# Ending the first block of a cross attention after one pair's key copies, and moving projection units one tile earlier in a wide attention

## The chip, the cores and the metric

The kernel runs on one core of a Trainium2 chip as a single program. The metric is the device time of one execution in microseconds; the time of a version is the median over several executions. Besides those, one execution was profiled; all views below read that one.

## The reference, cut to what matters

A perceiver-like stack of two layers over x (16 batches of 64 tokens, 256 features). Layer 0 does a cross attention to a context of 1601 rows with 16 heads of 16, then a "wide" attention with 8 heads of 128 over 1024 tokens and 1024 context rows, then a feed-forward with merged task weights. Layer 1 does a shared-key cross attention, an attention with position slopes, and a mixture of experts. Only these two attentions are touched:

```python
# cross attention, per batch of 64 tokens and per head (16 of 16 features)
qh = split(layernorm(x) @ wq + bq);  kh = split(ctx @ wk + bk);  vh = split(ctx @ wv + bv)
out = softmax(qh @ kh.T / 4) @ vh;   x = x + out @ wo + bo
# wide attention, per head (8 of 128 features), all 1024 tokens against all 1024 context rows
qh = split(layernorm(x) @ Wq);  kh = split(context @ Wk);  vh = split(context @ Wv)
sim = (qh @ kh.T) * 128 ** -0.5;  sim = (sim - mean(sim)) * 1.5 + mean(sim)
x = x + softmax(sim) @ vh @ Wout + bout
```

## The kernel before, in words

Every stage of the kernel is a block (`core.block()`, line 47) that holds one hand-written program for each engine: SyncE issues the transfers, TensorE multiplies, VectorE, ScalarE and GpSimd do the rest, and semaphores order them. A block ends when all its engine programs have ended; no engine starts the next block earlier. A transfer that was only issued need not have landed by then; who needs it waits on its semaphore.

**Cross attention** (`cross_attention_block`). `first_block` (line 556) normalises x, projects the queries of all batches, stores them to a scratch tensor in DRAM, and makes the keys and values of batch 0 in 17 projection units: 8 units of keys (4 for each of two groups of 4 head pairs), 7 of values, one of keys shared with layer 1, one that turns these. For each unit TensorE fills a PSUM bank (`project`), VectorE moves it out (`move_projection`), and for keys GpSimd splits it into a rounded and a rest part (`split_keys`). SyncE then copies the parts from SBUF to SBUF into the stacked layout `k_stack` (`stack_keys(n)`, line 446, four transfers of 200 KB for one head pair n; there are 8 pairs), and the queries into `q_stack` (`load_q`, line 439, eight transfers of 32 KB for one batch). `store_shared` (line 452) is eight transfers, `load_ctx` and `store_values` one each.

The main block then runs over 16 batches. In batch b TensorE goes through the 8 pairs; per pair it computes scores in two halves, turns the probabilities of the pair before, and does two projection units of batch b+1 in between. Each projection needs the bank `projected` moved out before. VectorE runs through the same order: maximum of the first score half, move of unit 2n, maximum of the second half, move of unit 2n+1. The move of the first key unit of a group overwrites `k_part`, from which `stack_keys` copies, and so waits until all four pairs of that group are stacked (in `move_projection`):

```python
if s == 0 and b > 0:
    for pair in range(GROUP_PAIRS * g, GROUP_PAIRS * (g + 1)):
        dve.wait_ge(k_stacked[pair], 64 * b)
```

**Wide attention** (`wide_attention_block`, line 1040). Eight heads one after the other; a head has eight tiles of 128 tokens (t = 0 to 7), and queries, keys and values of head h+1 are projected in six units (two of queries, two of keys, two of values) while head h runs. TensorE's order in tile t is: scores of t; at t = 1 the weighing of the last four tiles of the head before, at t = 5 that of the first four of its own (`weigh`); from t = 2 on unit t-2; then the turn of tile t-1's probabilities. VectorE: maximum of t; keeping what was weighed (t = 1 and 5); `normalise(t)`, which waits for ScalarE's exponential of t; from t = 2 on the move of unit t-2. ScalarE: exponential of t, then the copy of turned tile t-1. All six units share one bank, so unit u+1 waits for the move of u, and a head starts with a wait for the move of its own last unit: `pe.wait_ge(projection_moved, U * h + U)`. `over_heads` (line 1080) writes out heads 0, 1, 6 and 7 and runs heads 2 to 5 as a hardware loop of two rounds with two heads each; SyncE's weight loads are a loop of three rounds.

Of the kernel before, what the change touches and what calls it, by code (L numbers as in the profile page):

```python
# [26 lines left out]
PAIRS = HEADS // 2  # L27
GROUP_PAIRS = 4
# [356 lines left out]
def cross_attention_block(core, layer, x, wo, wk, wv, bk, bv, bo, w_shared, b_shared, scratch, heads_t):  # L385
# [15 lines left out]
    with ExitStack() as stack:  # L401
# [33 lines left out]
        def load_ctx(sp, b, parity):  # L435
            sp.dma_start(ctx[parity][:], dram["ctx_t"][ds(b, 1)].rearrange("o p c n -> (o p) c n")).then_inc(ctx_loaded[parity], 16)

        def load_q(sp, b, parity):
            for copy in range(COPIES):
                for e in range(2):  # L440
                    row = copy * PAIR_ROWS + e * HEAD_DIM
                    sp.dma_start(q_stack[parity][row:row + HEAD_DIM, :, e, :].bitcast(F32),
                                 scratch[copy // 2].rearrange("c (p e d) n -> e d (c p) n", e=2, d=HEAD_DIM)[e, :, :, ds(b * SEQ, SEQ)]
                                 ).then_inc(q_loaded[parity], 16)
# [111 lines left out]
        def first_block(first):  # L556
# [34 lines left out]
            with core.block() as block:  # L591
                @block.sync
                def _(sp):
                    for i in range(HALVES):
                        half = slice(i * TILES // 2, (i + 1) * TILES // 2)
                        sp.dma_start(x[:, half], dram["x"][:, half]).then_inc(x_loaded[i], 16)
                    sp.dma_start(core.ident[:], dram["ident"]).then_inc(ident_loaded, 16)
                    sp.dma_start(wk[:], dram[f"{layer}_wk"]).then_inc(keys_loaded, 16)
                    sp.dma_start(bk[:], dram[f"{layer}_bk"]).then_inc(keys_loaded, 16)
                    sp.dma_start(w_shared[:], dram["L1_xattn_wkv"]).then_inc(keys_loaded, 16)  # L600
                    sp.dma_start(b_shared[:], dram["L1_xattn_bkv"]).then_inc(keys_loaded, 16)
                    load_ctx(sp, 0, 0)
                    sp.dma_start(wq[:], dram[f"{layer}_wq"]).then_inc(query_loaded, 16)
                    sp.dma_start(bq[:], dram[f"{layer}_bq"]).then_inc(query_loaded, 16)
                    sp.dma_start(wv[:], dram[f"{layer}_wv"]).then_inc(values_loaded, 16)
                    load_ctx(sp, 1, 1)
                    for tile, view in ((core.even_head, dram["even_head"]), (core.odd_head, dram["odd_head"]), (bv, dram[f"{layer}_bv"]),
                                       (wo, dram[f"{layer}_wo"]), (bo, dram[f"{layer}_bo"].partition_broadcast(P))):
                        sp.dma_start(tile[:], view).then_inc(others_loaded, 16)
                    for i, (m, half) in enumerate(q_units):  # L610
                        for part, ready in ((0, high_ready), (1, low_ready)):
                            sp.wait_ge(ready, i + 1)
                            sp.dma_start(scratch[part, m, :, half * BANK:(half + 1) * BANK],
                                         parts[part][:, m, half * BANK:(half + 1) * BANK].bitcast(F32)).then_inc(query_stored, 16)
                    sp.wait_ge(zeros_ready, 4)
                    sp.wait_ge(query_stored, 16 * 2 * len(q_units))
                    load_q(sp, 0, 0)
                    load_q(sp, 1, 1)
                    for n in range(PAIRS):
                        if n % GROUP_PAIRS == 0:  # L620
                            sp.wait_ge(keys_split, CHUNKS_PER_GROUP * (n // GROUP_PAIRS + 1))
                        stack_keys(sp, n)
                        if n == GROUP_PAIRS - 1:
                            store_shared(sp, 0)
                    sp.wait_ge(projection_done, U)
                    load_ctx(sp, 2, 0)
                    store_values(sp, 0, 0)
                    sp.wait_ge(others_loaded, 16 * 5)

                @block.gpsimd  # L630
# [148 lines left out]
        with core.block() as block:  # L779
            @block.sync  # L780
            def _(sp):
                def batch(b, parity, ctx_left, q_left):

                    for n in range(PAIRS):
                        if n % GROUP_PAIRS == 0:
                            sp.wait_ge(keys_split, K_UNITS * (b + 1) + CHUNKS_PER_GROUP * (n // GROUP_PAIRS + 1))
                        sp.wait_ge(scored, 2 * (PAIRS * b + n + 1))
                        stack_keys(sp, n)
                        if n == GROUP_PAIRS - 1:
                            store_shared(sp, b + 1)  # L790
                    if q_left:
                        load_q(sp, b + 2, parity)
                    if ctx_left:
                        sp.wait_ge(projection_done, U * (b + 2))
                        load_ctx(sp, b + 3, 1 - parity)
                    store_values(sp, b + 1, 1 - parity)

                for b in range(BATCH - 1):
                    batch(b, b % 2, b < BATCH - 3, b < BATCH - 2)
                sp.wait_ge(shared_stored, 2 * CHUNKS_PER_GROUP * 16 * BATCH)  # L800
                for i in range(2):
                    sp.wait_ge(values_stored[i], 8 * BATCH)
# [237 lines left out]
def wide_attention_block(core, xn_t, ctx, w_q, w_k, w_v, wout, bout, heads_t):  # L1040
# [6 lines left out]
    with ExitStack() as stack:  # L1047
# [29 lines left out]
        weighed_ready = sem("weighed_ready")  # L1077
        heads_ready = sem("heads_ready")

        def over_heads(eng, body):  # L1080
            body(0, 0, True, False)
            body(1, 1, False, False)
            with eng.Fori(1, WIDE_HEADS // 2 - 1) as j:
                body(2 * j, 0, False, False)
                body(2 * j + 1, 1, False, False)
            body(WIDE_HEADS - 2, 0, False, False)
            body(WIDE_HEADS - 1, 1, False, True)

        with core.block() as block:
            @block.sync  # L1090
            def _(sp):
                def load(h, parity):
                    for tile, name in ((w_q, "L0_attn_wq"), (w_k, "L0_attn_wk"), (w_v, "L0_attn_wv")):
                        sp.dma_start(tile[parity][:], dram[name][ds(h, 1)].rearrange("o p c n -> (o p) c n")).then_inc(weights_loaded[parity], 16)

                sp.dma_start(bout[:], dram["L0_attn_bout"].partition_broadcast(P)).then_inc(out_loaded, 16)
                sp.dma_start(wout[:], dram["L0_attn_wout"]).then_inc(out_loaded, 16)
                with sp.Fori(0, WIDE_HEADS // 2 - 1) as j:
                    for parity in range(2):
                        used = sp.snap(U * (2 * j + parity + 1))  # L1100
                        sp.wait_ge(projection_done, used)
                        load(2 * j + parity + 2, parity)
                sp.wait_ge(out_loaded, 32)

            @block.gpsimd
# [5 lines left out]
            def _(pe):  # L1111
# [49 lines left out]
                def head(h, parity, first, last):  # L1161
                    pe.wait_ge(projection_moved, U * h + U)
                    for t in range(TILES):
                        score(h, parity, t)
                        if t == 1 and not first:
                            weigh(h - 1, 1 - parity, 1)
                        if t == QUERY_TILES + 1:
                            weigh(h, parity, 0)
                        if not last and 2 <= t:
                            project(h + 1, 1 - parity, t - 2)  # L1170
                        if t > 0:
                            turn(h, t - 1)
                        elif not first:
                            turn(h - 1, TILES - 1)

                for u in range(U):
                    project(0, 0, u)
                over_heads(pe, head)
                turn(WIDE_HEADS - 1, TILES - 1)
                weigh(WIDE_HEADS - 1, 1, 1)  # L1180

# [1 line left out]
            def _(dve):  # L1183
# [34 lines left out]
                def head(h, parity, first, last):  # L1218
                    for t in range(TILES):
                        maximum(h, t)  # L1220
                        if t == 1 and not first:
                            keep_heads(h - 1, 1)
                        if t == QUERY_TILES + 1:
                            keep_heads(h, 0)
                        normalise(h, t)
                        if not last and 2 <= t:
                            move_projection(h + 1, 1 - parity, t - 2)

                for u in range(U):
                    move_projection(0, 0, u)  # L1230
                over_heads(dve, head)
                keep_heads(WIDE_HEADS - 1, 1)

            @block.scalar
            def _(act):
# [21 lines left out]
                        elif not first:  # L1257
                            move_turned(h - 1, TILES - 1)

                over_heads(act, head)  # L1260
                move_turned(WIDE_HEADS - 1, TILES - 1)


# [1393 lines left out]
```

## Time and profile before

| | us |
|---|---|
| median of 3 executions | 2504.31 (2503.99 to 2508.21) |
| the profiled execution, its own time | 2509.65 |
| its span in the trace | 2507.8 |
| first block of the cross attention ends on TensorE's side | about 49 |
| main block of the cross attention starts | about 81 |
| wide attention's block, first scores to last weighing | 960.9 to about 1350 |

The span is what the trace covers; 1.85 us of the execution's own time lie around it. "PE" is TensorE's matmuls, "PEld" its weight loads, "DVE" VectorE, "ACT" ScalarE, "POOL" GpSimd, "SPq" the issue of transfers by SyncE. A matmul group "x4" for two matmuls in the code is what fp32 operands cost in passes. In a timeline the first number is the start, the second how long the merged group lasted, and square brackets tell how long the engine had been idle and who released it.

### The profile page before, as it was taken

The numbers are of one execution on the slowest core, as the hardware profiler recorded it, in microseconds if no ns is written. First come the engines' busy times: TensorE is split into PE (matmuls) and PEld (weight loads), VectorE is DVE, ScalarE is ACT, GpSimd is POOL, SyncE is SP. The second block draws the span as 40 slices with busy tenths as digits, with TensorE's granted clock in tenths as the row PEclk, the third lists the DMA queues.
The fourth block names the chain that finished last, engine by engine and source line by source line (L and its number), as shares of the span: only waits on it lengthen the run. The fifth ranks groups of instructions, "written<-read, shape, count | busy, mean of one in ns | idle before, by whom it ended". The sixth has DMA issues, their size and how long they took to land. (4 is left out here: it accounts for less than half of the span.)

```text
span 2507.8 us, 39287 instructions
## 1 busy us (share of the span) xinstructions
PE 2203.5 (88%) x15444; PEld 1472.6 (59%) x15444; DVE 1261.2 (50%) x2221; ACT 1000.1 (40%) x1861; POOL 310.8 (12%) x353
## 2 busy tenths in 40 slices
PE   5699999999999878999998799958999997685694
PEld 3477777777777754455555587834555544444463
DVE  3455665656566534454442344356777734564113
ACT  1355555555555533333331011115666653241221
POOL 2233222232223100000000000050000001000102
PEclk9899999999999969999999799968999999795897
DMA  6667777677777600000000312051222203115112
GB/s 186 139 144 180 177 179 172 154 180 179 180 162 167 146 23 26 11 6 5 5 1 1 125 69 100 18 104 22 26 31 34 34 1 86 39 18 209 61 45 67
DMA packets 107749, 220.09 MB, mean 88 GB/s; under 512 B 58818, under 2 KB 75211, under 8 KB 101844
## 3 DMA queue, kind: packets, MB, share of 16 engines
q1 hardware_dynamic: 106036, 213.44, 35.5%
q0 software_dynamic: 1536, 4.20, 0.5%
q8 instruction: 122, 2.00, 0.3%
q14 instruction: 55, 0.45, 0.1%
HBM read 91.08 MB, written 19.27 MB: 44 GB/s over the span
## 5 line engine op out<-in xcount | busy, mean ns | idle before, releaser
L905 DVE TENSOR_REDUCE L_xattn_maxima<-L_xattn_scores 128x1 f32<-128x1024 f32 (+1 forms) x256 | 253.7, 991 | 245.5 <-PE L_xattn_scores L828 245.0
L972 ACT ACTIVATE L_xattn_probs_t<-L_xattn_turned 128x1024 f32<-128x1024 f32 (+1 forms) x256 | 220.6, 862 | 339.1 <-PE L_xattn_turned L840 339.1
L1763 DVE TENSOR_REDUCE shared_half_maxima<-shared_ring 128x1 f32<-128x1024 f32 (+1 forms) x256 | 248.9, 990 | 107.0 <-PE shared_ring L1677 103.4
L1836 ACT ACTIVATE shared_exps<-shared_scores 128x512 f32<-128x512 f32 (+1 forms) x416 | 225.6, 594 | 123.6 <-PE shared_scores L1698 122.9
L984 ACT ACTIVATE L_xattn_probs<-L_xattn_scores,L_xattn_maxima 128x1024 f32<-128x1024 f32 (+1 forms) x256 | 235.4, 925 | 38.0 <-DVE L_xattn_maxima L908 38.0
L840 PE MATMUL L_xattn_turned<-ident,L_xattn_probs 128*128 128x128 f32 x1664 | 236.2, 282 | 12.2 <-ACT L_xattn_probs_t L972 11.2
L840 PEld LDWEIGHTS L_xattn_turned<-ident,L_xattn_probs 128*128 128x128 f32 x1664 | 199.1, 145 | 79.4 <-issue 46.7
L828 PE MATMUL L_xattn_scores<-L_xattn_k_stack,L_xattn_q_stack 128*128 128x512 f32 (+1 forms) x512 | 160.9, 396 | 50.7 <-DVE L_xattn_fold L958 33.2
L506 PE MATMUL L_xattn_projected<-L_xattn_wv,L_xattn_ctx 128*128 128x256 f32 x780 | 193.6, 389 | 0.0
L500 PE MATMUL L_xattn_projected<-L_xattn_ctx,L_xattn_wk 128*128 128x400 f32 x480 | 182.3, 502 | 0.0
L1698 PE MATMUL shared_scores<-shared_q,shared_k 128*128 128x512 f32 (+1 forms) x416 | 154.7, 450 | 7.3 <-DMA shared_q<-shared_max_rows 7.1
L1677 PE MATMUL shared_ring<-shared_k,shared_q 128*128 128x512 f32 (+1 forms) x512 | 139.8, 374 | 22.1 <-DMA shared_q<-q_scratch 12.8
L506 PEld LDWEIGHTS L_xattn_projected<-L_xattn_wv,L_xattn_ctx 128*128 128x128 f32 x780 | 137.2, 187 | 21.3 <-issue 0.3
L1252 ACT ACTIVATE wide_probs<-wide_scores,wide_stats 128x1024 f32<-128x1024 f32 x64 | 71.3, 1114 | 163.6 <-DVE wide_stats L1202 163.6
L469 POOL CAST L_xattn_k_part<-L_xattn_k_part 128x400 fp32r<-128x400 f32 (+1 forms) x128 | 66.2, 517 | 555.6 <-DVE L_xattn_k_part L530 555.6
L1379 PE MATMUL ffn_merging<-ffn_spread,ffn_task 128*128 128x256 f32 x512 | 129.5, 404 | 5.0 <-DVE ffn_merged L1458 5.0
L471 POOL TENSOR_TENSOR L_xattn_k_part<-L_xattn_k_part 128x400 fp32r<-128x400 f32 (+1 forms) x128 | 132.6, 1036 | 10.2
L1712 PE MATMUL shared_weighed<-shared_exps,shared_v 128*32 128x256 f32 (+1 forms) x1664 | 132.9, 391 | 0.2 <-ACT shared_exps L1836 0.2
L1137 PE MATMUL wide_scores<-wide_k_t,wide_q_t 128*128 128x512 f32 x256 | 122.2, 600 | 11.3 <-DVE wide_v L1192 11.3
L1677 PEld LDWEIGHTS shared_ring<-shared_k,shared_q 128*128 128x128 f32 x512 | 98.0, 201 | 48.2 <-DVE shared_half_maxima L1763 16.9
L828 PEld LDWEIGHTS L_xattn_scores<-L_xattn_k_stack,L_xattn_q_stack 128*128 128x128 f32 x512 | 79.6, 196 | 77.5 <-issue 42.8
L1157 PE MATMUL wide_weighed<-wide_probs_t,wide_v 128*128 128x512 f32 x256 | 116.0, 607 | 10.3 <-ACT wide_probs_t L1243 10.3
(368 smaller groups left out, 3065.4 us busy)
## 6 DMA issues: line engine op xcount, KB each, us to landing
L_xattn_k_stack<-L_xattn_k_part SPq DMA_DIRECT2D x512, 200.2 KB, 4.2
L_xattn_ctx<-in_ctx_t SPq DMA_DIRECT2D x16, 1602.0 KB, 6.9
ffn_task<-in_ffn_task SPq DMA_DIRECT2D x16, 1024.0 KB, 6.7
experts_w_in<-in_expert_in SPq DMA_DIRECT2D x8, 1024.0 KB, 11.6
shared_k<-k_scratch SPq DMA_DIRECT2D x64, 100.1 KB, 4.2
L_xattn_q_stack<-q_scratch SPq DMA_DIRECT2D x128, 32.0 KB, 2.0
k_scratch<-L_xattn_shared_part SPq DMA_DIRECT2D x128, 32.0 KB, 1.7
shared_q<-q_scratch SPq DMA_DIRECT2D x64, 64.0 KB, 4.6
```

The source lines that it names most:

```text
L500: last = nc.tensor.matmul(bank[:, 0:w], wk[:, k, g * P:(g + 1) * P], ctx[parity][:, k, s:s + w], start=k == 0, stop=k == CHUNKS - 1)
L506: last = nc.tensor.matmul(bank[0:rows, i * DIM:(i + 1) * DIM], ctx[parity][:, k, t * P:t * P + rows], wv[:, k, :], start=k == 0, stop=k == ...
L828: last = nc.tensor.matmul(scores[:, s // BANK, 0:w], q_stack[parity][:, n].rearrange("p h q -> p (h q)"), k_stack[:, n, s:s + w], start=Tr ...
L840: last = nc.tensor.transpose(turned_tiles[:, i, :], probs[n % 2][:, t * P:(t + 1) * P], core.ident[:])
L905: nc.vector.reduce_max(maxima[n % 2][:, half:half + 1], cols, axis=AX).then_inc(halves_maxed, 1)
L972: nc.scalar.activation(probs_t[:, t:t + m, p * P:(p + 1) * P], turned_tiles[:, 0:m, :], ACT.Copy).then_inc(turned_moved, 1)
L984: nc.scalar.activation(probs[n % 2][:, lo:hi], scores_flat[:, lo:hi], ACT.Exp, bias=maxima[n % 2][:, 2:3], scale=SCALE, accum_out=sums[n / ...
L1677: last = nc.tensor.matmul(ring[:, s // BANK, 0:w], q[slot][:, 2 * n:2 * n + 2, :].rearrange("r h q -> r (h q)"), k[slot][:, s:s + w], star ...
L1698: nc.tensor.matmul(scores[0:m, h, :], k[slot][:, t * P:t * P + m], q[slot][:, h * 8:(h + 1) * 8, :].rearrange("r h q -> r (h q)"), start=T ...
L1712: last = nc.tensor.matmul(weighed[b % 2][32 * c:32 * (c + 1), 0, 0:TILE_COLS], v[0:m, b, t, :], exps[n % 2][0:m, c * TILE_COLS:(c + 1) * T ...
L1763: nc.vector.reduce_max(half_maxima[:, n, half:half + 1], ring_flat[:, HALF_STARTS[half]:HALF_STARTS[half + 1]], axis=AX).then_inc(ring_max ...
L1836: nc.scalar.activation(exps[n % 2][0:m, h * BANK:(h + 1) * BANK], scores[0:m, h, :], ACT.Exp, scale=SCALE).then_inc(exps_done, 1)
```

## The change

In the cross attention, the SyncE program of the first block now ends after the queries of batch 0 and the keys of the first pair are on their way. The stacking of pairs 1 to 7, the shared store, the queries of batch 1, the context of batch 2 and the store of the shared values are issued at the start of SyncE's program in the main block, in this new order.

In the wide attention, projection unit t-1 is done in tiles 1 to 6 (before: unit t-2 in tiles 2 to 7), ahead of the weighing in that tile; VectorE moves it right after the maximum, ahead of keeping the weighed tile and of `normalise`. The loops over heads and over weight loads are written out for all engines.

```diff
@@ first_block, SyncE
                     load_q(sp, 0, 0)
-                    load_q(sp, 1, 1)
-                    for n in range(PAIRS):
-                        if n % GROUP_PAIRS == 0:
-                            sp.wait_ge(keys_split, CHUNKS_PER_GROUP * (n // GROUP_PAIRS + 1))
-                        stack_keys(sp, n)
-                        if n == GROUP_PAIRS - 1:
-                            store_shared(sp, 0)
-                    sp.wait_ge(projection_done, U)
-                    load_ctx(sp, 2, 0)
-                    store_values(sp, 0, 0)
+                    sp.wait_ge(keys_split, CHUNKS_PER_GROUP)
+                    stack_keys(sp, 0)
                     sp.wait_ge(others_loaded, 16 * 5)
@@ main block, SyncE
+                for n in range(1, PAIRS):
+                    if n == GROUP_PAIRS:
+                        store_shared(sp, 0)
+                        sp.wait_ge(keys_split, K_UNITS)
+                    stack_keys(sp, n)
+                load_q(sp, 1, 1)
+                sp.wait_ge(projection_done, U)
+                load_ctx(sp, 2, 0)
+                store_values(sp, 0, 0)
                 for b in range(BATCH - 1):
@@ wide attention, over_heads
-        def over_heads(eng, body):
-            body(0, 0, True, False)
-            body(1, 1, False, False)
-            with eng.Fori(1, WIDE_HEADS // 2 - 1) as j:
-                body(2 * j, 0, False, False)
-                body(2 * j + 1, 1, False, False)
-            body(WIDE_HEADS - 2, 0, False, False)
-            body(WIDE_HEADS - 1, 1, False, True)
+        def over_heads(body):
+            for h in range(WIDE_HEADS):
+                body(h, h % 2, h == 0, h == WIDE_HEADS - 1)
@@ SyncE
-                with sp.Fori(0, WIDE_HEADS // 2 - 1) as j:
-                    for parity in range(2):
-                        used = sp.snap(U * (2 * j + parity + 1))
-                        sp.wait_ge(projection_done, used)
-                        load(2 * j + parity + 2, parity)
+                for h in range(2, WIDE_HEADS):
+                    sp.wait_ge(projection_done, U * (h - 1))
+                    load(h, h % 2)
@@ TensorE, head
                         score(h, parity, t)
+                        if not last and 1 <= t <= U:
+                            project(h + 1, 1 - parity, t - 1)
                         if t == 1 and not first:
                             weigh(h - 1, 1 - parity, 1)
                         if t == QUERY_TILES + 1:
                             weigh(h, parity, 0)
-                        if not last and 2 <= t:
-                            project(h + 1, 1 - parity, t - 2)
@@ VectorE, head
                         maximum(h, t)
+                        if not last and 1 <= t <= U:
+                            move_projection(h + 1, 1 - parity, t - 1)
                         if t == 1 and not first:
                             keep_heads(h - 1, 1)
                         if t == QUERY_TILES + 1:
                             keep_heads(h, 0)
                         normalise(h, t)
-                        if not last and 2 <= t:
-                            move_projection(h + 1, 1 - parity, t - 2)
```

## Rows read from the trace of the kernel before

**Rows 1.** The page, busy time of each engine and its share of the span.
```profile
PE 2203.5 (88%) x15444; PEld 1472.6 (59%) x15444; DVE 1261.2 (50%) x2221; ACT 1000.1 (40%) x1861; POOL 310.8 (12%) x353
```

**Rows 2.** Timeline around the block boundary: start, duration, engine, line, what.
```profile
49.20 0.16 DVE L553 COPY L_xattn_v_shared<-L_xattn_first_projected 65x16 f32<-65x16 f32 x1
...
81.12 0.48 DVE L956 MEMSET L_xattn_projected<- 128x512 f32 x1 [31.75 <-PEq L50]
...
82.09 1.19 PE L828 MATMUL L_xattn_scores<-L_xattn_k_stack,L_xattn_q_stack 128*128 128x512 f32 x2 [33.20 <-DVE L_xattn_fold L958]
...
85.99 0.63 DVE L530 TENSOR_SCALAR L_xattn_k_part<-L_xattn_projected,L_xattn_bk 128x400 f32<-128x400 f32 x1 [1.44 <-PE L_xattn_projected L500]
...
109.21 0.64 DVE L530 TENSOR_SCALAR L_xattn_k_part<-L_xattn_projected,L_xattn_bk 128x400 f32<-128x400 f32 x1
```

**Rows 3.** Timeline of SyncE's issues over the same boundary and into batch 0.
```profile
36.86 7.44 SPq L442 DMA_DIRECT2D L_xattn_q_stack<-q_scratch  x16
44.34 14.60 SPq L449 DMA_DIRECT2D L_xattn_k_stack<-L_xattn_k_part  x16
...
63.81 14.63 SPq L449 DMA_DIRECT2D L_xattn_k_stack<-L_xattn_k_part  x16
...
79.50 0.96 SPq L461 DMA_DIRECT2D v_scratch<-L_xattn_v_shared  x1
105.96 14.61 SPq L449 DMA_DIRECT2D L_xattn_k_stack<-L_xattn_k_part  x16
```

**Rows 4.** One tile's instructions, k_stack, in 44.2 to 54.6: twelve issues, and landing.
```profile
L449 SPq DMA_DIRECT2D L_xattn_k_stack<-L_xattn_k_part x12: 580/923/1024, 44.3 to 54.0; - x12
...
DMA to landing us min/median/max: 2.9/4.1/4.3
```

**Rows 5.** Timeline of TensorE in the wide attention, tiles inside heads and at head changes.
```profile
1120.01 1.88 PE L1137 MATMUL wide_scores<-wide_k_t,wide_q_t 128*128 128x512 f32 x4
1121.99 1.98 PE L1119 MATMUL wide_projected<-wide_xn_t,wide_w_q 128*128 128x512 f32 x4
...
1144.56 1.88 PE L1137 MATMUL wide_scores<-wide_k_t,wide_q_t 128*128 128x512 f32 x4
...
1150.92 1.98 PE L1137 MATMUL wide_scores<-wide_k_t,wide_q_t 128*128 128x512 f32 x4 [1.53 <-DVE wide_v L1192]
...
1156.78 7.13 PE L1157 MATMUL wide_weighed<-wide_probs_t,wide_v 128*128 128x512 f32 x16 [1.29 <-ACT wide_probs_t L1243]
...
1164.62 1.88 PE L1137 MATMUL wide_scores<-wide_k_t,wide_q_t 128*128 128x512 f32 x4
1166.34 1.88 PE L1119 MATMUL wide_projected<-wide_xn_t,wide_w_q 128*128 128x512 f32 x4
...
1205.62 7.13 PE L1157 MATMUL wide_weighed<-wide_probs_t,wide_v 128*128 128x512 f32 x16 [1.22 <-ACT wide_probs_t L1243]
...
1254.31 7.13 PE L1157 MATMUL wide_weighed<-wide_probs_t,wide_v 128*128 128x512 f32 x16 [1.14 <-ACT wide_probs_t L1243]
...
1302.99 7.13 PE L1157 MATMUL wide_weighed<-wide_probs_t,wide_v 128*128 128x512 f32 x16 [1.13 <-ACT wide_probs_t L1243]
```

**Rows 6.** Timeline of the last head, which projects nothing: tiles 2 to 4.
```profile
1310.84 1.88 PE L1137 MATMUL wide_scores<-wide_k_t,wide_q_t 128*128 128x512 f32 x4
...
1316.54 1.08 PE L1147 MATMUL wide_turned<-ident,wide_probs 128*128 128x128 f32 x8 [1.23 <-DVE wide_probs L1210]
1317.45 1.88 PE L1137 MATMUL wide_scores<-wide_k_t,wide_q_t 128*128 128x512 f32 x4
...
1319.00 1.01 ACT L1243 ACTIVATE wide_probs_t<-wide_turned 128x1024 f32<-128x1024 f32 x1
```

**Rows 7.** Timeline of TensorE in the first head, tiles 1 and 2.
```profile
966.64 1.74 PE L1147 MATMUL wide_turned<-ident,wide_probs 128*128 128x128 f32 x8 [2.02 <-DVE wide_probs L1210]
968.18 2.96 PE L1137 MATMUL wide_scores<-wide_k_t,wide_q_t 128*128 128x512 f32 x4
970.97 1.88 PE L1119 MATMUL wide_projected<-wide_xn_t,wide_w_q 128*128 128x512 f32 x4
```

More of the change, by code:

```diff
@@ L1177, in _ @@
                     project(0, 0, u)
-                over_heads(pe, head)
+                over_heads(head)
                 turn(WIDE_HEADS - 1, TILES - 1)
@@ L1225, in head @@
                         normalise(h, t)
-                        if not last and 2 <= t:
-                            move_projection(h + 1, 1 - parity, t - 2)
                 for u in range(U):
                     move_projection(0, 0, u)
-                over_heads(dve, head)
+                over_heads(head)
                 keep_heads(WIDE_HEADS - 1, 1)
@@ L1258, in head @@
                             move_turned(h - 1, TILES - 1)
-                over_heads(act, head)
+                over_heads(head)
                 move_turned(WIDE_HEADS - 1, TILES - 1)
```

## The prediction

> **What bounds the kernel now.** I read the page first: TensorE is busy 88% of the span [rows 1], and the stages run one after the other, so time can only come out of stretches in which TensorE stands. The timeline around the first boundary shows the largest: VectorE's last work of the first block ends at 49.36, the main block starts at 81.12, TensorE's first scores come at 82.09 after 33.2 us of nothing [rows 2]. SyncE's own timeline tells why: it issues transfers without a pause from 36.86 to 80.46, and the block ends 0.66 us later (81.12 less 79.50 and 0.96) [rows 2, 3]. So the boundary is set by SyncE's issuing, not by any result. In the wide attention the reader is to see short waits instead: 1.53 us at a head's start, for VectorE's move of the last value unit, and 1.29 us ahead of the weighing in tile 1, for ScalarE's copy [rows 5].
>
> **Part 1, the end of the first block.** SyncE now issues 8 query transfers instead of 16 and 4 key copies. From the rows the 8 take half of 7.44, to 40.6, and the first pair's four 3.7 at most (a quarter of 14.60), to 44.3 [rows 3]. The block then ends with VectorE, at 49.36; plus the same 0.66 the main block starts at 50.0, and by the same 0.97 TensorE's first scores at 51.0. That alone would be worth 31.1 us.
>
> But a wait takes over. VectorE's second instruction in batch 0 is the move of the first key unit of batch 1, into the buffer from which pairs 0 to 3 are copied, and it waits for all four to have landed. Before, pair 3 was issued by 58.94 and VectorE got there at 85.99 [rows 2, 3], so the wait cost nothing. Now pairs 1 to 3 are issued from 50.1 on. Twelve such issues go from 44.3 to the start of the last at 54.0, 9.7 us, and one takes 4.1 (at most 4.3) to land [rows 4]: 50.1 + 9.7 + 4.2 = 64.0, and the move starts at 64.1 instead of 85.99. Queued behind it are the maximum of the second score half, hence both exponentials, and on TensorE unit 1, which waits for the bank, and everything after it. So the main chain is 21.9 us early, not 31.1.
>
> Of this the clock takes something back. TensorE does one projection and the scores from 51.0 on, then stands for some 10 us until 64.7. In the trace, work right after an idle time of 2.0 us is at the lower level: from 966.64 to 970.97, 4.33 us for a turn and a score pair [rows 7], which warm take 0.91 (1316.54 to 1317.45) and 1.72 (1164.62 to 1166.34) [rows 5, 6], so 1.7 lost. Before, such a slow stretch lay ahead of 85.99, thus inside what is already counted; now one comes behind the move. I take 1.7, with 0 (the slow stretch falls into ScalarE's first exponential) and 3.5 (two such stretches) as ends. Part 1 gives 21.9 - 1.7 = 20.2 us, from 18 to 22.
>
> Is anything late next? The group-1 keys of batch 1 are moved at 109.21 [rows 2], now 89.0. They wait for pairs 4 to 7: SyncE is through pair 3 at 60.7, the shared store of 4.9 (58.94 to 63.81) brings it to 65.6, the 16 issues of 14.63 to 80.2 [rows 3], landed by 83.6: 5 us of slack. Then 8 query issues (3.7), the context and the values (78.44 to 80.46, 2.0) end at 85.9 [rows 3]. The next stacking, for batch 1, waited for GpSimd until 105.96 [rows 3], now 85.8, and so is not delayed by more than 0.2; its reader comes with batch 1, tens of us later. Every moved issue is thus under computation. If SyncE's issues were a fifth slower beside computing, group 1 would land near 88; still in time.
>
> **Part 2, the wide attention.** Take a change of heads, from tile 7's scores to the weighing in tile 1. Before: 1144.56 to 1156.78, 12.22 us, with one projection unit and both waits in it [rows 5]. After: tile 7 has no unit, its scores are followed by one turn and the next head's scores, which need wait no longer, since the last unit was moved in tile 6. But now the turn of tile 7 comes too soon for its own probabilities. The last head shows this very order without a projection: scores at 1310.84, turn of the same tile at 1316.54, 1.23 us of it idle; next scores at 1317.45 [rows 6]. So 5.70 + 0.91, then scores 1.72 and the unit that now stands in tile 1, another 1.72 [rows 5] (the unit's own length taken as that of the scores, four matmuls of the same shape): 10.05. ScalarE's copy for the weighing is done 9.17 us after the scores of tile 7 (1319.00 + 1.01 less 1310.84) [rows 6], hence hidden. Gain 2.17 us, at the six changes from head 0 to head 6.
>
> At the seventh, head 7 has no unit in tile 1: the weighing waits for that copy, at about 9.35, and the unit taken out of tile 7 (1.72) still has to be done before: 12.22 - 9.35 - 1.72 leaves 1.1 us.
>
> Bank waits inside a head: the second query unit began 1.98 after the scores instead of 1.72 (1120.01 to 1121.99) [rows 5], since VectorE moved the first behind `normalise`. Moved right after the maximum, this goes: 0.26 for each of seven heads, 1.8 us.
>
> Head 0 stands 2.02 us before its first turn and then runs slow, 1.7 us lost as above [rows 7]. The unit in tile 1 fills 1.6 of that idle time (the turn itself waits for VectorE's normalising and stays where it is), and with 0.4 idle the slow stretch should go: 3.3 us, or 1.6 if it stays.
>
> VectorE's order could cost: the move now stands ahead of `normalise`. But `normalise` waits for ScalarE's exponential, which can start only behind the maximum, and the move falls into that time. It lasts 0.63 for 400 columns [rows 2], by which I estimate 0.8 for 512. I count nothing; uncovered it would be up to 0.8 a tile (rival C).
>
> The loops: four heads change from loop to straight code. Inside the loop a head took 48.84 (1156.78 to 1205.62), outside 48.68 (1254.31 to 1302.99) [rows 5], 0.2 us apart, and this lies in the waits just removed: no term of its own, 0 to 0.8 us. The Trainium skill (Runtime: NRT & Kernel Launch, Instruction fetch mechanics) says that a taken branch out of the fetched window stalls until its page is fetched, and that prefetching is sequential; by it the written-out loop would gain, and the trace allows that at most these 0.2 us a head.
>
> Part 2: 6 x 2.17 = 13.0, + 1.1 + 1.8 + 3.3 = 19.2 us, from 15 to 21.
>
> **Sum.** 20.2 + 19.2 = 39.4 us off the profiled execution's 2509.65, 2470.3. The profiled one stood 5.3 us above the median; nothing in the removed time is particular to it, so the same is taken off the median: 2504.3 - 39.4 = 2464.9 us.
>
> **Rivals.**
> A: the wait for pairs 0 to 3 does not bind, and the whole 31.1 us come. For it: only that the boundary gap is that long. Against: the wait is in the code and the landing time in the rows. 2504.3 - 31.1 - 19.2 = 2454.0. 4%.
> B: TensorE's clock falls at the new wait ahead of tile 7's turn, at each of seven head changes. Each costs 1.7 [rows 7], 12 us in all: 2476.8. Against it: the last head has this wait of 1.23 us and behind it runs a turn in 1.08 and scores in 1.88, warm [rows 6]; idle times of 1.53 were followed by warm work too [rows 5]. 8%. The Trainium skill (TensorE: Matmul & The Clock Gate, "A second HAM failure mode: psum-queue depth-cycling") tells of frequent short idle times in which the clock keeps falling; that is this rival.
> C: VectorE is the bound in the wide attention once the waits on TensorE go: `normalise` behind move and maximum late by the whole move, 0.8 us, in each of 42 tiles with a unit, 34 us, of which TensorE's own work hides about half, so part 2 shrinks to about nothing: 2484. For it: VectorE's waits are chained tile to tile. Against: it waits for TensorE and ScalarE within each of these tiles. 6%.
> D: SyncE falls behind in batch 0 and stays there, so that the stacking for batch 1 comes after its scores would begin. It would take away half of part 1: 2475. The slack of 5 us speaks against it. 8%.
> E, the other side: straight code starves. Four more heads come from memory as fresh instructions on four engines. It turns the sum only if each costs 39.4 / 4 = 9.9 us more; heads 1 and 6 are straight code and are no slower than looped ones [rows 5]. By this, or by clock changes in later stages as large, 2510. 2%.
> That the change does nothing (the block's end set by something else than SyncE) would leave part 2 alone, 2485: 2%.
> The forecast itself, with its own range of 2460 to 2471: 70%.
>
> **How the numbers follow.** The forecast is the likeliest case, 2464.9. Range 2456 to 2479: from above rival A to above B and D, leaving out A, C, E and the idle change, 14%, and a little of the others. A difference under 0.2% (5 us) is about what measuring this kernel can't tell from no change. Faster by more than that: all but E and some of what I can't name, 97%; within it 1%; slower 2%.
>
> **What would show it.** The first block's end near 50, first scores at 51, then VectorE idle from about 53 to 64 with k_stack's transfers as releaser, then slow matmuls for some 4 us. Batch 0's move for group 1 starts near 89 instead of 109.21. In the wide attention: no idle time at a head's first scores nor before the weighing in tile 1 (but in head 7), and 1.2 us before the turn at each change of heads; a head of 46.4 us. Wrong would be: VectorE's move starting at 53 or after 66; a head above 47.5; key copies late for batch 1; or a lower clock where the new waits stand.

## The result, and the profile after

The changed kernel takes 2464.93 us (median of 4, 2464.0 to 2468.08) against 2504.15 us beside it. The ratio is 0.9844, 95% interval 0.9827 to 0.9861: 39.2 us less, between 35 and 43. The profiled execution took 2465.39 us, its span is 2463.5 us, 44.3 less than before.

The page's row of busy times. It answers to [rows 1]: TensorE did the same 15444 matmuls in 10 us less of busy time and stands less.

```profile
PE 2193.6 (89%) x15444; PEld 1469.8 (60%) x15444; DVE 1263.0 (51%) x2221; ACT 999.3 (41%) x1861; POOL 311.4 (13%) x353
```

The busy time by stretch, first of the kernel before, then of the changed one. The four stretches are cut at the same events in both: the first block until VectorE's last work in it; from there to VectorE's move of batch 1's first keys; the rest of the cross attention until the wide attention's first scores; the wide attention. The columns are start and end, length, busy time of each engine, TensorE's granted clock as a share of full speed, the share of the DMA engines and their GB/s.

```profile
0.00:49.36 49.36, 36.73 (x136) 23.19 (x136) 21.14 (x53) 6.41 (x10) 16.36 (x26) 1.00 0.55 184
49.36:85.99 36.63, 3.90 (x7) 2.42 (x8) 1.94 (x5) 0.00 (x0) 0.50 (x5) 0.54 0.91 212
85.99:960.93 874.94, 826.68 (x7411) 630.30 (x7410) 501.24 (x921) 460.02 (x776) 223.57 (x272) 0.97 0.67 152
960.93:1351.10 390.17, 360.79 (x1355) 196.53 (x1356) 180.60 (x313) 139.19 (x192) 0.00 (x0) 0.98 0.02 5
```

```profile
0.00:48.62 48.62, 36.12 (x136) 23.11 (x136) 21.15 (x53) 6.41 (x10) 16.37 (x26) 1.00 0.54 181
48.62:62.53 13.91, 3.70 (x8) 2.02 (x8) 1.94 (x4) 0.00 (x0) 0.51 (x5) 0.70 0.86 184
62.53:935.48 872.95, 825.48 (x7409) 628.73 (x7409) 501.13 (x921) 460.41 (x776) 223.98 (x272) 0.97 0.69 158
935.48:1305.40 369.92, 352.62 (x1355) 195.93 (x1356) 182.36 (x313) 137.76 (x192) 0.00 (x0) 0.99 0.02 6
```

The reader is to see two stretches that shrink: the second, 36.63 to 13.91 (22.7 us), and the fourth, 390.17 to 369.92 (20.25 us). The first, in which the programs do the same work until near its end, differs by 0.7 us, the third by 2.0 us.

The timeline behind the first block, of the changed kernel. It answers to [rows 2].

```profile
48.46 0.16 DVE L553 COPY L_xattn_v_shared<-L_xattn_first_projected 65x16 f32<-65x16 f32 x1
49.09 0.48 DVE L957 MEMSET L_xattn_projected<- 128x512 f32 x1 [0.47 <-PEq L50]
...
50.06 0.70 PE L829 MATMUL L_xattn_scores<-L_xattn_k_stack,L_xattn_q_stack 128*128 128x512 f32 x2 [1.91 <-DVE L_xattn_fold L959]
...
62.53 0.63 DVE L530 TENSOR_SCALAR L_xattn_k_part<-L_xattn_projected,L_xattn_bk 128x400 f32<-128x400 f32 x1 [10.51 <-DMA L_xattn_k_stack<-L_xattn_k_part]
...
63.22 3.63 PE L514 MATMUL L_xattn_projected<-L_xattn_ctx,L_xattn_w_shared 128*32 128x512 f32 x16 [9.46 <-DVE L_xattn_k_part L530]
...
66.81 1.18 PE L829 MATMUL L_xattn_scores<-L_xattn_k_stack,L_xattn_q_stack 128*128 128x512 f32 x2
```

The main block starts 0.47 us after VectorE's last work, and then VectorE stands 10.51 us, released by a transfer of `k_stack`. SyncE's own timeline answers to [rows 3]; the first line of key copies runs over the boundary and holds its wait:

```profile
36.11 3.64 SPq L442 DMA_DIRECT2D L_xattn_q_stack<-q_scratch  x8
39.80 19.52 SPq L449 DMA_DIRECT2D L_xattn_k_stack<-L_xattn_k_part  x16
59.36 4.72 SPq L456 DMA_DIRECT2D k_scratch<-L_xattn_shared_part  x8
64.13 14.54 SPq L449 DMA_DIRECT2D L_xattn_k_stack<-L_xattn_k_part  x16
79.09 4.49 SPq L442 DMA_DIRECT2D L_xattn_q_stack<-q_scratch  x8
83.63 0.43 SPq L436 DMA_DIRECT2D L_xattn_ctx<-in_ctx_t  x1
84.10 0.43 SPq L461 DMA_DIRECT2D v_scratch<-L_xattn_v_shared  x1
84.65 16.59 SPq L449 DMA_DIRECT2D L_xattn_k_stack<-L_xattn_k_part  x16
```

The wide attention's TensorE timeline at a change of heads, which answers to [rows 5], and in head 0, which answers to [rows 7]:

```profile
1014.38 1.95 PE L1122 MATMUL wide_projected<-wide_w_v,wide_ctx 96*128 96x128 f32 x16
1016.16 1.04 PE L1141 MATMUL wide_turned<-ident,wide_probs 128*128 128x128 f32 x8
1017.04 1.88 PE L1131 MATMUL wide_scores<-wide_k_t,wide_q_t 128*128 128x512 f32 x4
1018.76 1.04 PE L1141 MATMUL wide_turned<-ident,wide_probs 128*128 128x128 f32 x8
1019.63 1.88 PE L1131 MATMUL wide_scores<-wide_k_t,wide_q_t 128*128 128x512 f32 x4
1022.74 1.07 PE L1141 MATMUL wide_turned<-ident,wide_probs 128*128 128x128 f32 x8 [1.23 <-DVE wide_probs L1204]
1023.65 1.88 PE L1131 MATMUL wide_scores<-wide_k_t,wide_q_t 128*128 128x512 f32 x4
1025.37 1.88 PE L1113 MATMUL wide_projected<-wide_xn_t,wide_w_q 128*128 128x512 f32 x4
1027.09 7.03 PE L1151 MATMUL wide_weighed<-wide_probs_t,wide_v 128*128 128x512 f32 x16
```

```profile
935.48 3.70 PE L1131 MATMUL wide_scores<-wide_k_t,wide_q_t 128*128 128x512 f32 x8 [0.78 <-DVE wide_v L1186]
939.02 1.88 PE L1113 MATMUL wide_projected<-wide_xn_t,wide_w_q 128*128 128x512 f32 x4
941.19 1.10 PE L1141 MATMUL wide_turned<-ident,wide_probs 128*128 128x128 f32 x8 [0.29 <-DVE wide_probs L1204]
942.12 1.88 PE L1131 MATMUL wide_scores<-wide_k_t,wide_q_t 128*128 128x512 f32 x4
```

From tile 7's scores (1017.04) to the weighing (1027.09) it is 10.05 us, before 12.22. The only wait in it is the 1.23 us ahead of tile 7's turn, and what follows runs warm, that is, at TensorE's higher clock: scores in 1.88 us.

### The profile page after: what moved, and what is told of

It is laid out like the page before. It is cut to its first block and busy times, and to the rows that moved or that the text cites. A ratio compares the mean times of both kernels' runs of the same rounds, so it can differ in the third digit from the quotient of the medians.

```text
span 2463.5 us, 39049 instructions
## 1 busy us (share of the span) xinstructions
PE 2193.6 (89%) x15444; PEld 1469.8 (60%) x15444; DVE 1263.0 (51%) x2221; ACT 999.3 (41%) x1861; POOL 311.4 (13%) x353
## 5 line engine op out<-in xcount | busy, mean ns | idle before, releaser
L500 PEld LDWEIGHTS L_xattn_projected<-L_xattn_ctx,L_xattn_wk 128*128 128x128 f32 x480 | 91.0, 190 | 46.4 <-issue 0.6
```

Of the source, the lines that this page charges most:

```text
L500: last = nc.tensor.matmul(bank[:, 0:w], wk[:, k, g * P:(g + 1) * P], ctx[parity][:, k, s:s + w], start=k == 0, stop=k == CHUNKS - 1)
```

## The experiments

All were timed against the kernel before, in three groups, each on a chip of its own with its own runs of that kernel (medians 2508.2, 2506.75 and 2508.66 us). So the ratios are what can be compared between groups, and differences of medians within one.

**One part at a time.** The first block's change without the wide attention's:

> Only the first block's end is changed, the wide attention is as before. My theory (the wait for pairs 0 to 3 takes over from the block's end): VectorE's first move of batch 1's keys starts 13 to 15 us after the first block's last VectorE work instead of 36.6, and the time falls by 20 to 23 us, to about 2482. Rival (the block's end was all of it): 31 us, 2473. Rival (SyncE falls behind in the batches): 10 us or less.

Measured: 2487.09 against 2508.2 us, ratio 0.9921 (0.9906 to 0.9935), 21.1 us less by the medians, 16 to 24 by the interval. VectorE's last work ended at 48.75, its move of the first keys came at 62.74, 14.0 us later, released by a transfer of `k_stack`. The whole 31 us of the idle boundary would have been 0.9876, outside the interval. The rival in which SyncE falls behind is out as well.

The order in the wide attention alone, its loops kept and the first block as before:

> Only the order in the wide attention is changed, its hardware loops stay, and the first block is as before. My theory: heads of 46.4 to 46.6 us instead of 48.8, 18 to 20 us in all, to about 2485. Rival (the written-out loops are what gains): under 5 us.

Measured: 2490.01 against 2508.2 us, ratio 0.9924 (0.9911 to 0.9937), 18.2 us less, 16 to 22 by the interval. From weighing to weighing two by two a head took 46.35 to 46.43 us. The rival that the written-out loops gain is out: here there are none.

The loops alone, written out as in the change:

> Only the loops over heads and over weight loads are written out. My theory: 0.2 us for each of four heads, under 1 us in all, no difference that can be measured. Rival (taken branches cost more than the waits show): 3 us or more. Rival (straight code starves): slower.

Measured: 2508.83 against 2508.2 us, ratio 0.9998 (0.9989 to 1.0006). In its trace heads took 48.70 us, one of them 49.04 (its two halves 26.19 and 22.85), where in the loop they had taken 48.92 and 48.84 by turns. So by the traces the loops are worth less than 1 us in 2500, and by the time nothing that can be measured.

The medians of the two parts sum to 39.3 us less, and both together gave 39.2. So they add, though with intervals 6 to 8 us wide an agreement within 0.1 us is luck.

**The kernel before once more**, unchanged, one execution:

> The kernel before once more, for a second trace of it. Between the two traces now at hand, batches 1 to 15 of the cross attention differ by short idle times of TensorE that nothing releases, 1.4 to 2.3 us each, three in the one and one or two in the other. If they are chance, this trace has them at other places and its span is a few us off 2507.8; if they belong to the kernel before, they stand at the same places again.

Measured: 2506.6 us, span 2504.7. Again one idle time of TensorE of 1.16 us that nothing releases stood at batch 5 (here at 377.04, before at 379.83; the two experiments above that keep the old first block have one there too, at 380.35 and 376.36); others stood elsewhere or were missing. The answer is mixed: some of these idle times came again, others did not.

The same trace shows something about head 0 of the wide attention. TensorE stands 2.02 us before its first turn, as in the first trace [rows 7], but what follows is warm:

```profile
965.45 1.09 PE L1147 MATMUL wide_turned<-ident,wide_probs 128*128 128x128 f32 x8 [2.02 <-DVE wide_probs L1210]
966.38 1.88 PE L1137 MATMUL wide_scores<-wide_k_t,wide_q_t 128*128 128x512 f32 x4
```

The two experiments that keep the old order there, the first block alone and the loops alone, show the same (turns of 1.10 and 1.09 us behind 2.01 us of idle time). From the first scores to the weighing in tile 1 of head 1 it took 48.04 us in all three, and 49.17 in the first trace of the kernel before. So the slow work of [rows 7] was particular to that execution, and 1.1 us of it reached the stage's length.

**Is it the landing of pair 3 that sets the main chain?** The shared store is put ahead of pairs 1 to 3, so that these are later and nothing else is changed:

```diff
+                store_shared(sp, 0)
                 for n in range(1, PAIRS):
                     if n == GROUP_PAIRS:
-                        store_shared(sp, 0)
                         sp.wait_ge(keys_split, K_UNITS)
                     stack_keys(sp, n)
```

> The changed kernel, with the eight transfers of the shared store issued ahead of pairs 1 to 3 in the main block instead of behind them: the landing of pair 3 is later by their 4.7 us, nothing is taken out or added. Theory (that landing sets the main chain): VectorE's first move at 67.2 instead of 62.5 and the whole kernel slower by 4.7 us. Rival (the move has slack): no difference from the changed kernel.

The eight transfers took 3.6 us to issue here, not 4.7. The timeline of this run, its move and the first scores:

```profile
48.40 0.16 DVE L553 COPY L_xattn_v_shared<-L_xattn_first_projected 65x16 f32<-65x16 f32 x1
...
66.36 0.63 DVE L530 TENSOR_SCALAR L_xattn_k_part<-L_xattn_projected,L_xattn_bk 128x400 f32<-128x400 f32 x1 [14.40 <-DMA L_xattn_k_stack<-L_xattn_k_part]
...
70.63 0.98 PE L829 MATMUL L_xattn_scores<-L_xattn_k_stack,L_xattn_q_stack 128*128 128x512 f32 x2
```

The move came 17.8 us after the first block's end instead of 13.9, and every weighing of the cross attention from the first to that of batch 11 was 3.7 to 3.8 us later than in the changed kernel's trace. So the landing does set the chain. The time does not show it: 2467.09 us (2460.46 to 2475.54) against 2468.46 for the changed kernel in the same group. The trace, taken of the fastest of these five executions, tells how such a shift can be lost. Past batch 11 the changed kernel's own trace has an unreleased idle time of 2.15 us at 713.95 that this one doesn't have, and between 840 and 890, in the last batches, the granted clock was 0.67 there (0.71 in its repeat) and 0.80 here. So the wide attention's first weighing came 3.3 us earlier here (955.28 against 958.56), not later.

**How many pairs should the first block stack?** Three, and all four of the group:

```diff
                     sp.wait_ge(keys_split, CHUNKS_PER_GROUP)
-                    stack_keys(sp, 0)
+                    for n in range(3):      # 4 in the other version
+                        stack_keys(sp, n)
@@ main block
-                for n in range(1, PAIRS):
+                for n in range(3, PAIRS):   # 4
```

> The changed kernel, but three pairs are stacked in the first block instead of one. Two limits set VectorE's first move: the landing of pair 3, and the block's end plus 3 to 5 us of first scores and projection. Theory: twelve issues from 39.8 end near 50.5, the main block starts at 51.2 (changed kernel: 49.1), pair 3 lands at 57 to 58, and the move starts there instead of 62.5: 4.5 to 5 us less than the changed kernel, 2460. Rival (only the block's end counts, as I would have it if the wait for the pairs were a side effect): 2 us more, 2467.

> The changed kernel, with all four pairs of group 0 stacked in the first block, so that VectorE's move has no wait for pairs behind the boundary. Theory: SyncE ends near 54.4, the main block starts at 55.1, scores at 56, and the move comes 3.9 us later, as in the kernel before, at 59.9, by then bound by the block's end: 2.5 us less than the changed kernel, 2 us more than with three pairs. Rival (the wait for pairs is all): 57.7, better than three pairs.

The timelines, with three pairs and then with four: VectorE's last work of the first block, its first of the main block, and the move.

```profile
48.32 0.16 DVE L553 COPY L_xattn_v_shared<-L_xattn_first_projected 65x16 f32<-65x16 f32 x1
51.09 0.48 DVE L958 MEMSET L_xattn_projected<- 128x512 f32 x1 [2.61 <-PEq L50]
...
57.56 0.63 DVE L530 TENSOR_SCALAR L_xattn_k_part<-L_xattn_projected,L_xattn_bk 128x400 f32<-128x400 f32 x1 [3.05 <-DMA L_xattn_k_stack<-L_xattn_k_part]
```

```profile
49.28 0.16 DVE L553 COPY L_xattn_v_shared<-L_xattn_first_projected 65x16 f32<-65x16 f32 x1
56.11 0.48 DVE L958 MEMSET L_xattn_projected<- 128x512 f32 x1 [6.68 <-PEq L50]
...
60.99 0.64 DVE L530 TENSOR_SCALAR L_xattn_k_part<-L_xattn_projected,L_xattn_bk 128x400 f32<-128x400 f32 x1 [1.44 <-PE L_xattn_projected L500]
```

The releaser in the brackets changes: with three pairs it still is a transfer, with four it is TensorE's projection, which waited for the block's end. From VectorE's last work to the first batch's first weighing's last products it took 46.0 us in the changed kernel, 41.9 with three pairs, 43.2 with four, and 68.2 in the kernel before. In time they are alike (three pairs, then four): 2461.18 and 2460.17 against 2506.75 us, ratios 0.9810 (0.9796 to 0.9825) and 0.9814 (0.9801 to 0.9828). The 1.3 us between them (43.2 less 41.9) is under what the timing tells. By the ratios both are 5 to 9 us faster than the changed kernel (0.9844 and, timed again, 0.9836), with intervals that touch or overlap its; the traces show 4.2 and 2.9 us in this stretch. With four pairs the price of the later first scores came back in part: TensorE was warm by the next pair's scores (0.70 against 1.20 us).

**The move's place on VectorE.** TensorE's order stays new, the move goes back behind `normalise`:

```diff
                         maximum(h, t)
-                        if not last and 1 <= t <= U:
-                            move_projection(h + 1, 1 - parity, t - 1)
 ...
                         normalise(h, t)
+                        if not last and 1 <= t <= U:
+                            move_projection(h + 1, 1 - parity, t - 1)
```

> The changed kernel, but VectorE moves a unit behind normalise, as before the change, while TensorE's order stays the new one. Theory (the unit's earlier place on TensorE gains most of it, the earlier move only the waits for the bank): 0.26 us back at two to four units of a head, heads of 46.9 to 47.4 instead of 46.35, 4 to 7 us slower than the changed kernel. Rival (the move's place was nearly all of it): heads of 48 or more, 12 us slower. Rival (the move's place costs normalise time, so late is better): faster.

Measured: 2470.58 against 2508.66 us, ratio 0.9845 (0.9831 to 0.9858), beside 2468.46 for the changed kernel. By the trace a head took 22.18 + 24.89 = 47.07 us. So the move's place is worth 0.7 us a head, and TensorE's new place for the units the other 1.8 or so of the 2.5 us that a head gained. In head 0 the late move costs 2.0 us, and the stage as a whole took 368.84 us from its first scores to the start of its last weighing, 6.1 more than in the changed kernel (362.74). By the time alone, 2.1 us by the medians, the two can't be told apart.

**Is the new 1.23 us wait worth removing?** The units stand in tiles 1, 2, 3, 4, 6 and 7, so that tile 7 has one again, but is moved early:

```diff
+    UNIT_AT = {1: 0, 2: 1, 3: 2, 4: 3, 6: 4, 7: 5}
 ...
-                        if not last and 1 <= t <= U:
-                            project(h + 1, 1 - parity, t - 1)
+                        if not last and t in UNIT_AT:
+                            project(h + 1, 1 - parity, UNIT_AT[t])
 (the same for move_projection on VectorE)
```

> The changed kernel, but the six projection units stand in tiles 1, 2, 3, 4, 6 and 7 instead of 1 to 6, so that tile 7 has a unit again (moved right after the maximum, ahead of normalise). Theory: the unit fills TensorE's 1.23 us of idle time before the turn of tile 7, and the next head's scores find the last unit moved or nearly so; heads of 44.9 to 45.2 us instead of 46.35, 8 to 10 us less than the changed kernel, near 2456. Rival (the wait for the last unit's move comes back at the head's start, as before the change): heads of 46.3 or more, no gain.

Three weighings one after the other in its trace, of tile 5, of the next head's tile 1 and of its tile 5; no bracket means no idle time before:

```profile
1006.30 7.03 PE L1152 MATMUL wide_weighed<-wide_probs_t,wide_v 128*128 128x512 f32 x16
1029.00 7.03 PE L1152 MATMUL wide_weighed<-wide_probs_t,wide_v 128*128 128x512 f32 x16
1051.39 7.03 PE L1152 MATMUL wide_weighed<-wide_probs_t,wide_v 128*128 128x512 f32 x16
```

A head took 45.1 us (1006.30 to 1051.39), 1.25 less than in the changed kernel, and TensorE was busy in all of it (45.09 of 45.09 us): the wait is gone and none has taken its place. Measured: 2457.6 against 2506.75 us, ratio 0.9799 (0.9785 to 0.9814), which lies wholly below the changed kernel's 0.9827 to 0.9861.

**Both on top of the change**, three pairs and the units in tiles 1 to 4, 6 and 7:

> Both edits on the changed kernel: three pairs in the first block, and the units in tiles 1 to 4, 6 and 7. Theory: they lie in different stages and add: 13 to 15 us less than the changed kernel, near 2451. Rival (one of them does nothing): 2456 to 2460.

Measured: 2453.05 us against 2506.75, ratio 0.9789 (0.9776 to 0.9803), its span 2447.2. In its trace the move came 9.1 us after the first block's last VectorE work (58.56 less 49.48) and a head took 45.1 us. It is the best version of this study, 12 to 14 us below the changed kernel by the ratios. Against the one with the units alone (0.9799) the 4.8 us by which the move came earlier (13.9 less 9.1) don't stand clear of the intervals.

**The changed kernel once more:**

> The changed kernel once more beside the others, for a second trace and an interval of its own: ratio to the kernel before 0.984 again, heads of 46.35 us, VectorE's first move near 62.5, and unreleased idle times of TensorE at other batches than in the first trace.

Measured: 2468.46 against 2508.66 us, ratio 0.9836 (0.9823 to 0.9850). The move came at 63.18, 13.9 us after the first block's last VectorE work as in the first trace; heads of 46.35 us. An unreleased idle time stood at 354.99 (1.69 us), where the first trace has none. The other one of the first trace, 2.15 us at 713.95, came again in the same batch (2.15 us at 718.79), against what was expected.

## Why the prediction was right

**The boundary.** It said that SyncE's issuing sets the block's end, that the boundary taken away would be worth 31.1 us alone, and that VectorE's wait for pairs 0 to 3 takes over. All three stand: the main block starts 0.47 us after VectorE's last work instead of 31.75, and the wait is there with the transfer as releaser, 10.5 us long. The experiment with the store ahead of the pairs, and those with three and four pairs, moved that wait as the working had it, within 1.1 us (66.36, 57.56 and 60.99). Forecast from the first block's end to the move: 14.7 us. Measured: 13.9. SyncE began to issue 0.3 us behind VectorE's last work instead of 0.7, and its twelve issues took 0.3 us less.

**The clock's term in part 1 was too large.** 1.7 us were taken off for slow work behind the move. The work was slow (3.63 us for the shared unit, 1.18 for the next scores; the granted clock from 62.53 to 66.81 was 0.50), but the shared unit lies beside ScalarE's first exponentials: from the move to the next pair's scores it is 4.28 us before (85.99 to 90.27) and 4.28 after (62.53 to 66.81). Only what comes behind was late: the first weighing's end was 22.9 us earlier (117.58 to 94.65) where the move was 23.5 earlier, so 0.5 us. That is near the lower end given for this term. The Trainium skill (TensorE: Matmul & The Clock Gate, "Part 1: The HAM clock gate") has the array at half rate behind idle time; the trace agrees behind the 9.46 us of this place, and shows besides that what this costs depends on what other engine is waited for meanwhile. Behind the 2.02 us of head 0 the clock fell in one of four traces; what decides it, no run here shows.

**What would be late next.** Nothing was. The group-1 keys moved at 86.28 (forecast 89.0), issues of their pairs ended at 78.67. SyncE was free for batch 1's stacking at 84.53, 1.5 us after GpSimd's last split (ends 83.00), where the working allowed 0.2; the chain in front had come earlier than counted. Its readers came tens of us later.

**The wide attention.** 10.05 us at a change of heads, forecast and measured. The turn's wait of 1.23 us came at every change as read from the last head, and the clock did not fall there, so rival B is out. A head of 46.35 (forecast 46.4). At the seventh change the weighing came 9.23 us after tile 7's scores (forecast 9.35). The stretch as a whole gave 20.2 us, forecast 19.2; the last turn of the stage, warmer in this trace (1.24 us against 1.95, but 1.96 with the order alone changed), gave 0.7 of the difference. VectorE did not become the bound (rival C): moving later was no faster. The loops gave 0.4 us by the traces (forecast 0 to 0.8).

**What was wrong in it.** The prediction took what it read from the profiled execution off the median as well, since "nothing in the removed time is particular to it". One thing was: the slow work in head 0, for which it counted 1.7 us. In the changed kernel the turn took 1.10 and the scores 1.88, where [rows 7] have 1.74 and 2.96, but three other traces with the old order have 1.09 or 1.10 and 1.88 too. Against those three the stage gave 18.8 to 19.1 us (381.50 to 381.89 less 362.74), not 20.2. Nor is work behind 2 us of idle time always slow, and the 1.7 us of both clock terms and of rival B were read from that one place.

**The sum.** By stretches the two traces give 22.2 us (the first weighing, measured from the first block's end) and 20.2 us, 42.4; the medians give 39.2, and the two parts alone 21.1 and 18.2. The forecast's 39.4 sits on the medians partly by luck: by these two traces it was 3 us short, 2 in part 1 (0.8 the move, 1.2 the clock) and 1 in part 2. Of the 3 us, 1.1 are head 0's slow work in the one execution. Where the medians lose the other 2 is not settled; the interval reaches 4 us to either side. The trace's own 44.3 us are those 42.4 and what three stretches with the same work differed by: 0.7 us in the first block, 2.5 from the first weighing to the wide attention, and 1.4 the other way behind the wide attention's last weighing.

## What to carry to other kernels

When a block ends with the queue of one engine that only issues transfers, the time of the gap is not the gain of closing it: look up who waits for those transfers first thing in the next block, and compute when the last of them lands. Then choose how many to issue ahead of the boundary: look for the number at which the landing and the block's end meet. Here that is three or four pairs; the traces favour three by 1.3 us, the time does not tell them apart.

In a software pipeline, filler work is worth most in the steps where the chain through the other engines is longest, and the place to read that from is a stretch of the same trace in which the filler is missing anyway, as the last head here. Taking the unit out of tile 7 only moved the wait, to that tile's turn (1.23 us); leaving tile 5 empty, which has a weighing of 7.03 us to fill it, instead of tile 7 took 1.25 us more off a head.

## What the runs showed that was not expected

TensorE has idle times of 1.2 to 2.2 us that no semaphore explains, almost all in the weighing of the cross attention, a run of many narrow matmuls. In the 13 traces of this study (both kernels twice and nine variants) those of over 1 us stand in the weighings of three batches: of batch 1 in four traces, of batch 5 in six, of batch 12 in seven (batches counted from 0). Only one other was seen, 1.16 us ahead of a turn at 562.96, with the units in tiles 1 to 4, 6 and 7; three traces have none at all. So where they can stand seems to belong to the program, and whether one comes, to the execution. What they are was not found out.

They are one reason why single traces differ. From the first weighing's last products to the wide attention's first scores no variant changes what TensorE does, and still this stretch took 833.7 to 845.6 us. The last batch, in which the granted clock differs (0.67 against 0.80 above), took 48.9 to 53.5 of it. So a shift of 3.8 us that a trace shows plainly at the place where it arises need not show in the medians of five executions.
